# Every layer in two halves of its tokens: attention of the second half beside the first half's projection, the feed-forward by halves

## The reference

```python
x = x + attn_a(layernorm(x))        # causal, 16 heads of 16; x@W1+b1, softmax(mask), @Wp+bp
x = x + ffn(layernorm(x))           # silu(x@wg.T) * (x@wu.T) @ wd.T, hidden 768, int weights / 127
x = x + attn_b(layernorm(x))        # window of 64 keys, 63 given keys ahead of the first token
x = x + ffn(layernorm(x))
# attn_a: w = einsum('bhqd,bhkd->bhqk', q, k) / 4; softmax over the keys up to the query
# attn_b: k_win = k_pad[:, idx] with idx = arange(l)[:, None] + arange(64)[None, :]
```

## Time and profile before

| | us |
|---|---|
| median of 3 runs | 1554.76 (1550.01 to 1557.61) |
| profiled execution, own time | 1558.07 |
| its span in the trace | 1556.3 |
| PE busy / DVE / ACT / POOL | 1312.2 / 965.1 / 756.2 / 390.9 |
| mean granted clock of TensorE | 0.932 of full speed |

### The profile page before, as it was taken

How to read it: one execution, slowest core, us unless ns; L and a number is a source line. 1 busy time by engine, 2 the same in 40 slices (tenths; PEclk the granted TensorE clock), 3 DMA queues, 4 the chain that set the end, 5 groups by cost and what they waited for, 6 DMA issues and landing times.

```text
span 1556.3 us, 23982 instructions
## 1 busy us (share of the span) xinstructions
PE 1312.2 (84%) x9473; PEld 813.8 (52%) x9473; DVE 965.1 (62%) x1564; ACT 756.2 (49%) x1133; POOL 390.9 (25%) x387
## 2 busy tenths in 40 slices
PE   2799879796998987989699997898788988798968
PEld 2533338654763325855584332784477333386547
DVE  5487655556567746555658773665556876555563
ACT  2426654344434675536342667453544266544534
POOL 1302223201330223311242123330134022232013
PEclk9979999998988999999796999999999699999979
DMA  7620120714170021152325011142235201207120
GB/s 290 203 66 16 60 78 30 188 37 139 49 191 2 23 97 62 52 138 73 136 61 145 9 60 62 54 129 63 91 116 138 68 16 57 74 38 186 57 85 28
DMA packets 86335, 134.86 MB, mean 87 GB/s; under 512 B 24176, under 2 KB 59312, under 8 KB 82992
## 3 DMA queue, kind: packets, MB, share of 16 engines
q1 hardware_dynamic: 86208, 133.09, 28.7%
HBM read 51.45 MB, written 11.61 MB: 41 GB/s over the span
## 4 chain that ended last, share of the span: by engine, by line
PE 56%; DVE 20%; ACT 8%; DMA 6%; issue 4%; POOL 4%; SPq 1%; POOLq 0%; ACTq 0%; DVEq 0%
DVE peak L594 13%; PE opsum L1072 11%; PE ring L1045 8%; PE ring L1022 6%; PE ring L1106 6%; PE ring L1107 6%; PE ring L990 5%; ACT probs L835 4%; PE opsum L1120 2%; PE opsum L1123 2%; DMA q_st<-peak_b 2%; PE ring L924 2%; PE ring L925 2%; PE ring L926 2%; PE ring L910 2%
## 5 line engine op out<-in xcount | busy, mean ns | idle before, releaser
L835 ACT ACTIVATE probs<-ring 128x768 f32<-128x768 f32 (+5 forms) x496 | 400.5, 836 | 403.6 <-PE ring L1045 252.2
L594 DVE TENSOR_REDUCE peak<-ring 128x4 f32<-128x768 f32 (+7 forms) x480 | 462.2, 1004 | 166.7 <-PE ring L990 163.5
L1022 PE MATMUL ring<-k_st,q_st 96*128 96x192 bf16 (+4 forms) x1280 | 275.9, 323 | 36.1 <-DVE peak L594 24.4
L1045 PE MATMUL ring<-q_st,k_st 98*128 98x512 bf16 (+5 forms) x1344 | 249.9, 296 | 47.6 <-DMA q_st<-peak_b 24.8
L1072 PE MATMUL opsum<-probs,V 128*32 128x192 f32 (+5 forms) x2816 | 223.6, 411 | 11.1 <-POOL probs L516 9.0
L1045 PEld LDWEIGHTS ring<-q_st,k_st 98*128 98x128 bf16 x1344 | 94.4, 99 | 204.7 <-ACT probs L835 65.9
L1022 PEld LDWEIGHTS ring<-k_st,q_st 96*128 96x128 bf16 x1280 | 99.1, 101 | 159.8 <-DVE peak L594 76.8
L516 POOL TENSOR_SCALAR_AFFINE_SELECT probs<-probs 128x512 f32<-128x512 f32 x128 | 81.2, 634 | 391.1 <-ACT probs L835 391.1
L528 POOL TENSOR_TENSOR h_lo<-hid,h_hi 128x512 fp32r<-128x512 f32 x96 | 123.4, 1289 | 205.1 <-ACT h_hi L869 205.1
L1106 PE MATMUL ring<-xt_hi,w_gu_sb 128*128 128x512 f32 x384 | 154.9, 403 | 21.7 <-issue 18.9
L990 PE MATMUL ring<-mask_a,ident_b 128*128 128x128 bf16 (+2 forms) x704 | 159.9, 280 | 0.0
(11 more groups left out here) (123 smaller groups left out, 1914.7 us busy)
## 6 DMA issues: line engine op xcount, KB each, us to landing
w_gu_sb<-img_gu SPq DMA_DIRECT2D x16, 1536.0 KB, 6.7
w_qkv<-img_qkv SPq DMA_DIRECT2D x8, 1536.0 KB, 7.5
q_st<-q_part SPq DMA_DIRECT2D x96, 128.0 KB, 2.5
q_st<-q_part SPq DMA_DIRECT2D x48, 256.0 KB, 4.6
on_hi<-o_hi SPq DMA_DIRECT2D x64, 128.0 KB, 2.7
k_st<-k_part SPq DMA_DIRECT2D x48, 144.0 KB, 2.5
k_st<-k_part SPq DMA_DIRECT2D x24, 288.0 KB, 7.3
k_st<-k_part SPq DMA_DIRECT2D x48, 128.0 KB, 2.5
```

Of the source, the lines that this page charges most:

```text
L594: dve.tensor_reduce(peak[:, g % 2, :].rearrange("p (h i) -> p h i", i=NT)[:, h:h + heads, i], heads_of(plan.slot[e], unit, plan.a_width(i) ...
L835: act.activation(probs[:, j % 2, h:h + heads, 0:w], heads_of(plan.slot[e], unit, w), ACT.Exp).then_inc(exp_done, 1)
L1022: pe.matmul(flat(plan.slot[e])[:, per * n + c:per * n + c + d], q, k_st[0:SP_ROWS, HG * g + h0 + n, first_key + c:first_key + c + d], star ...
L1045: last = pe.matmul(flat(plan.slot[e])[:, per * n + c:per * n + c + d], kk, q_st[:, HG * g + h0 + n, q0 + c:q0 + c + d], start=(per * n % 5 ...
```

## The change

The unit of attention is now a supergroup (`sg`, 0 to 7): 4 heads and half of the tokens as queries. Groups of the first half come first. In the causal layer the first half sees key tiles 0 to 3, the second all eight; in the sliding layer 0 to 4 (64 rows of tile 4) and 4 to 8.

- `opsum` has one bank per supergroup, by turns. The direct normalisation D is gone: every supergroup goes C, R, M, H, K. `probs` tiles are half as wide.
- N cuts the peaks into a bfloat16 part and a rest before the transpose, so T needs one DVE instruction and one DMA instead of two of each. The values V of four tiles, the projection of four tiles and the residual of two tiles are one unit each, in slots of the ring.
- O of the first half (`O0`) stands inside the attention of the second half. After attention come L2 (transposes for the first half's LayerNorm), gate and up of the first half (G0 to G5), `O1`, down of the first half (W), L3, gate and up of the second half (G6 to G11). Down of the second half is moved into the next layer as `w`, behind its first two Q.
- The order is made by a new `Plan.order`, a list scheduler with a table of durations (`steps`) and one of preferences (`LIKES`), one program for each engine apart. It also fixes which banks of the ring an event gets. PE waits for the earlier holders of exactly these banks.
- ACT's table loads are placed where the next operation of another table follows.

PE at the end of the first sliding layer, before: the last second-pass unit of group 3 (score matmul L1045, mask L990), the weighting by V (L1072), and the first projection tile (L957 to L959).

The diff, cut to its core:

```diff
 RING = 3
-V_FIRST = 4
+SUPERS = 2 * GROUPS
+USES_RING = "QPATBOLG"
+LIKES = (
+    dict(T=1.0, N=1.0, V=0.53, O=0.11, L=0.02, w=2.0, W=0.3, Z=0.15, H=0.26, M=0.77, J=0.05, I=0.2,
...
-        _, self.events = min((self.order(lead) for lead in ahead), key=lambda x: x[0])
+        self.us, self.program, self.banks = self.order(LIKES[0 if self.causal else 1])
...
+    def steps(self, e):
...
+            return [("PE", 0.03 + mask * heads + 0.00043 * w, 0.1), ("DVE", 0.09 + 0.00104 * w, 0.1)]
...
+        if kind == "V":
+            return [("PE", 0.1 + 0.00105 * self.b_width(e[1] // 4, e[2]), 0.15)]
+        if kind in "wW":
+            return [("PE", 4.4, 0.1), ("DVE", 2.1 if self.causal == (kind == "W") else 0.7, 0.1)]
...
+        if kind == "G":
+            k = e[1]
+            gate = [(("I", k - 2), 0)] if k >= 2 else [(("V", 7, self.keys[1][-2]), 0)]
+            return [[(("L", 2 + k // 6), 2), (last_b, 0), (("F", "gu", 1), 0)], gate][step]
...
+                    elif kind == "N":
...
+                        dve.tensor_copy(peak_h[:], peak[:, sg % 2, 0, :]).then_inc(peak_cut, 1)
+                        dve.wait_ge(peak_cut, n + 1)
+                        dve.tensor_tensor(peak[:, sg % 2, 1, :], peak[:, sg % 2, 0, :], peak_h[:],
+                                          ALU.subtract).then_inc(peak_lo, 1)
...
-                    elif kind == "D":
...
-                        dve.reciprocal(osb[:, k, :], osb[:, k, :]).then_inc(direct, 1)
...
+            def slot_free(a, e):
+                for b, (kind, *n) in BEFORE[a, e]:
...
+                    elif kind == "A":
+                        pe.wait_ge(a_max, A_BASE[b] + plan.a_base[n[0]] + n[1] + 1)
...
-                for t in range(4, NT):
-                    project(a, t)
-                    if t == 5:
-                        turn(0, 2 * a + 1)
...
-                pe.wait_ge(gu_in, 32 * (a + 1))
-                for k in range(12):
-                    gate_up(k)
...
-                    if k >= 9:
-                        down(k - 9)
...
+            work = [(a, e) for a in range(LAYERS) for e, step in PLANS[a].program["PE"]]
+            first = [work.index((a, ("G", 0))) for a in range(LAYERS)]
+            last = [work.index((a + 1, ("w", 1, 1))) + 1 for a in range(LAYERS - 1)] + [len(work)]
+            done = 0
+            for n0, n1 in zip(first, last):
+                run(work[done:n0])
                 with pe.If(has_second > 0):
+                    run(work[n0:n1], True)
                 with pe.Else():
+                    run(work[n0:n1], False)
+                done = n1
```

More of the change, by code:

```diff
@@ L695, in _ @@
+            dve.wait_ge(x_in, 16)
+            for m in range(2):
+                for p in range(2):
+                    stats_of(m, p, x_next)
             for n, (_, _, ints) in enumerate(weights):
@@ L761, in _ @@
             for a in range(LAYERS):
-                attention(a)
-                ffn(a)
+                layer(a)
         @block.scalar
@@ L1143, in _ @@
             pe.wait_ge(s_pool, 3)
-            for h in range(2):
-                turn(h, 0)
+            for m in range(2):
+                turn(m, m)
             pe.wait_ge(s_split, 2)
```

1548 lines of the change are left out of this document (849 added, 699 removed), and 5 rows, old and new, of the table w.

## The result

| | before | changed kernel |
|---|---|---|
| median of the runs, us | 1554.82 (1550.01 to 1557.61, 4 runs) | 1571.36 (1568.18 to 1573.12, 4 runs) |
| ratio, 95% interval | | 1.0105 [1.0087, 1.0124] |
| profiled execution, its span | 1558.07, 1556.3 | 1573.12, 1571.4 |
| mean granted clock | 0.932 | 0.949 |
| PE idle (span less busy) | 244.1 | 259.8 |

What follows compares the result with a forecast made beforehand. PE was taken to bound about 1312 us, the rest serial hand-overs at layer seams. Gains of 14 us a sliding and 9 a causal layer, 4 x 23 = 92, took the 1556.3 us span to 1464, put down as 1460, range 1430 to 1490.

Steps and rivals of the forecast that it cites:

- the seam's timetable behind G0: Sliding seam: G0 5.2 us after last V, six G units (9.9 us) cover normalisation, then O1 and W; 9.2 us gained.
- the sliding layers' first scores: Sliding start: two moved down tiles cover the split-and-stack chain, ready about 12.1 us after first Q; PE idle 0.8 us.
- Sliding middle: Saturated stage of sliding attention: pays for 4 extra B units and 4 extra V tiles, 2 us lost.
- they only move: Sliding start: two deferred down-projections, 6.0 us, only move from one layer's end to the next layer's start.
- Causal tail: Causal layer after the last reduction: 20 us of ACT with O0 beside it, 21 us instead of 33.
- The causal middle: Causal attention between start and last reduction: between 106 and 128 us from PE's and DVE's work, taken as 115.
- rival A: Only the seams gain: DVE bounds the causal middle at 128 us instead of 115; 1512 us, chance 0.22 with E.
- Rival D: PE at 1.2 GHz through first halves, +17 us a causal layer; 1528 us, chance 0.05.
- C: Slower: PE waits for slots fixed by a table of assumed durations, 0.54 us a stop; 1590 us, chance 0.08.
- E: Halves do not overlap, O0 and its LayerNorm come late: seam gains about half, 1500 us; chance 0.22 with A.
- The sign set for a wrong forecast: Seam after attention: forecast is wrong if first-half work is spread so that G0 waits over 8 us after last V.
- The clock: Sliding seam stages, granted 0.79 and 0.80 of full speed: less idle there gains some 1.4 us a layer.

Runs made afterwards that it cites:

- h2: Changed kernel with Sqrt table loaded by the root, causal slots renamed, second-half LayerNorm scale and L3 sooner (causal), first q parts sooner (sliding): 1518.70 us, ratio 0.9754.
- f7: Changed kernel with the LayerNorm root's Sqrt table loaded by the root itself, not ahead: 1548.04 us, ratio 0.9963 to the kernel before.
- g3: Changed kernel with the second half's LayerNorm scale and L3 moved sooner in the causal layers: 1565.19 us, ratio 1.0063 to the kernel before.
- f5: Changed kernel with the LayerNorms' square root replaced by a copy and its table loads dropped (output differs): 1547.94 us, ratio 0.9954 to the kernel before.
- e3: Changed kernel with the first half's projection held until after all attention, order made anew: 1615.58 us, ratio 1.0410 to the kernel before.
- h3: h2 with e3's edit, the first half's projection held until after all attention: 1600.14 us, ratio 1.0283 to the kernel before.
- e2: Changed kernel with two slots of the later causal layers renamed, so the first Q does not take L5's: 1557.52 us, ratio 1.0025 to the kernel before.
- g1: Changed kernel with the L2 transposes moved ahead of the last V tiles in every layer: 1576.51 us, ratio 1.0140 to the kernel before.
- h4: h2 plus g1's move of L2, with another slot for L2 in the causal layers: 1515.32 us, ratio 0.9733 to the kernel before.

## Why the prediction was wrong

It expected to gain 92 us in eight layers, and the kernel lost 15 in its trace. By its own stages, from first Q to first exponential, to last reduction, to last V, to next Q (forecast from its working, then the changed kernel, then the four edits of h2):

| us | forecast | changed | h2 |
|---|---|---|---|
| causal: start | 32.0 | 35.9 | 34.9 |
| causal: middle | 115 | 113.3 | 115.5 |
| causal: tail | 21 | 25.1 | 25.0 |
| causal: seam | 39.7 | 45.1 | 40.9 |
| sliding: start (38.8 + 6.0 - 5.4) | 39.4 | 42.8 | 40.9 |
| sliding: middle, with O0 (55.1 + 2 + 2.9) | 60 | 66.2 | 66.1 |
| sliding: seam (64.8 - 6.0 - 2.9 - 9.2 - 1.4) | 45.3 | 50.9 | 42.0 |
| pair | 352 | 379.3 | 365.3 |

The sliding seam's forecast comes out of a difference of totals; by the prediction's own clock times (G6 at 27.4, six units, two transposes) it would be about 39. The layers of h2 (columns as in the earlier trace rows):

```profile
776.10:992.40 216.30, 189.01 (x1252) 101.48 (x1251) 139.18 (x216) 118.01 (x155) 60.36 (x63) 0.96 0.23 70
992.40:1141.40 149.00, 131.89 (x1142) 98.35 (x1141) 85.95 (x184) 76.87 (x122) 35.69 (x30) 0.95 0.34 103
```

**The step that failed: the seam's timetable behind G0** ("Six G units (9.9 us, to 15.1) then cover"). In us after the end of the last V tile, over all eight layers:

| | forecast | changed | h2 |
|---|---|---|---|
| G0 starts | 5.2 | 3.9 to 4.7 | 3.9 to 4.4 |
| six G units last | 9.9 | 12.3 to 13.8 | 12.3 to 13.7 |
| first down starts | 18.0 | 21.9 to 23.6 | 20.4 to 22.1 |
| G6 starts, causal | 27 | 31.7 to 34.4 | 27.2 to 27.6 |
| G6 starts, sliding | 27.4 | 31.3 to 34.7 | 29.9 to 31.7 |

G0 came as forecast. The stop before G6, forecast at 3 and 3.4 us, is 2.5 us in the causal layer and 1.5 in the sliding one. What was put at nothing, or too short, is this:

- The six G units. 9.9 is six times 1.65, the planner's own duration for a unit; at full clock a unit takes 1.82 us in the trace, and behind the stop before G0 the first matmuls run at the lower level of the clock (below).
- The stop before down, 2.4 us, at nothing. 1.5 us of it go when the table load goes from ahead of ACT's copies (f7). The forecast counted the two loads in the causal tail as part of ACT's 20 us, and no other.
- The 4.0 us before the first Q of the later causal layers, at nothing. The forecast spoke of table-given slots for the scores, and here it is the first Q.
- The 4.4 us before the sliding layers' first scores, at 0.8. The stack was there 15.9 us after the first Q and not 12.1.

The working followed one chain and let every other queue be free.

The runs show 23 us for where the loads stand, 14 for the slot and 6 for the root's result waiting in DVE's list, 53 together, against the 111 missed. In the traces (1571.4 to 1520.0 us) 35.8 of them are idle time of PE and 15.6 its busy time, so the clock has a share in each of these prices. In h2 the seams are at 40.9 and 42.0, the causal one 1.2 over its forecast and the sliding one 3.3 under. That closeness is in part luck: the stop before G6 that g3 removes was in the forecast, 3 us a causal layer, and it makes up for six G units that still last 2.4 us or more over the forecast. What was right in the mechanism is that the overlap removes the wait for the projection and that G0 follows the last V tile closely.

**Sliding middle**, 6 us a layer. The forecast charged 2 us for added units. One part is first-pass units that moved. The reductions of the sliding layer by stage, of the kernel before (start, rest) and of the changed one:

```profile
1023.70:1062.50 38.80, 13.21 (x15) 0.97 0.75 189
1062.50:1117.60 55.10, 16.28 (x17) 0.96 0.16 52
```
```profile
1024.50:1067.30 42.80, 7.48 (x8) 0.88 0.41 114
1067.30:1133.50 66.20, 22.78 (x24) 1.00 0.35 106
```

Before, 15 of 32 first-pass units ran in the start, where PE had time; now 8 do, since two supergroups are two half groups. Seven more stand in the middle, at about 0.66 us of PE each (four scores and a mask; an estimate from their distance in the trace), 4.6 us. The step "they only move" was applied to down and not asked of the first pass. But PE's busy time there is 60.31 us, hardly more than the 59.5 that the forecast's 60 contains (its idle time of 0.55 taken off); the stage is granted 1.00 for 0.96 before, which gives some of it back. What the stage has more than forecast is idle time, 5.9 us for 0.55 before: it is not saturated any more. 5.8 of them PE waits before V tiles for exponentials, 15 times, and 2.0 at once behind the two table loads, which f5 takes away.

**Causal tail**, 4 us. Ahead of it ACT is done with supergroup 6, and the last group's first exponential needs transposed peaks, their cut, one DMA and the scores:

```profile
953.03 1.23 DVE L760 TENSOR_REDUCE peak<-ring 128x1 f32<-128x1024 f32 x1 [0.64 <-PE ring L1126]
```
```profile
957.68 0.62 ACT L1017 ACTIVATE o_hi<-onf 128x512 fp32r<-128x512 f32 x1
961.43 2.85 ACT L998 ACTIVATE probs<-ring 128x1024 f32<-128x1024 f32 x3 [3.13 <-PE ring L1170]
```

7.2 us lie between the last reduction and that exponential, and ACT stands for 3.13 of them. The forecast counted ACT's work alone, and ACT's work is as forecast: 19.91 busy us for 20. So the 4 us are ACT's idle time, most of it this hop, and no run took it away. The two table loads among the 20 are worth 2.5 us or so: without them, in f5, the tail is 22.4 us. h2 leaves them where they are, and its tail is 25.0.

**What held.** Waits before the projection vanished, for both halves. The causal middle, the term with the widest bounds, came out at 113.3 for 115: rival A (128, DVE-bound) is refuted, with DVE at 89.75 of 113.30, 0.79. (A's 128 rests on DVE's work of about 110 us; the terms listed for it add up to 106. The three attention stages measured 113.) Rival D too: the four causal starts are granted 0.90 to 0.95 and the middle read here 1.00 (the first 38 us of one other middle 0.88). Nor did C's stops come: PE's own waits of the first-pass scores on "probs" and "peak" are 22.3 and 15.4 us, for 7.5 and 24.4 before, 6 us more in all. (The 76.8 of the earlier trace rows that C priced a stop by is the weight load's wait, PEld; PE's own was 24.4, 60 times.) But C had named the right object, slots given by a table, at the wrong instruction, and the result lies in C's direction. E did not happen, and e3 shows roughly what it would have cost. The sign set for a wrong forecast, G0 over 8 us after the last V tile, did not show although the forecast was wrong; the sliding layer at 159.9 for 145 and the idle time at 259.8 for 150 did.

**The clock**, priced at 1.4 us a sliding layer and at nothing in the causal one, is worth more than that. Behind the 2.46 us stop before G0 shown above, the matmuls of gate and up first follow each other at 0.43 us and then at 0.23:

```profile
985.20 0.63 PE L1237 MATMUL ring<-xt_lo,w_gu_sb 128*128 128x512 f32 x1
985.62 0.63 PE L1236 MATMUL ring<-xt_hi,w_gu_sb 128*128 128x512 f32 x1
...
988.09 0.40 PE L1236 MATMUL ring<-xt_hi,w_gu_sb 128*128 128x512 f32 x1
988.33 0.39 PE L1237 MATMUL ring<-xt_lo,w_gu_sb 128*128 128x512 f32 x1
```

The granted clock is 0.53 from 983.78 to 987.20 and 1.00 from there to 996.20; at the sliding seam it is 0.50 for 6.1 us. At its two levels, the mean granted clock says how long the slow one ran: 2 x (1 - 0.949) x 1571 = 160 us in the changed kernel, 116 in h2 (0.962), 221 in h3 (0.931). From h2 to h3 the slow time grows by 105 us, PE's busy time by 31.4 and its idle time by 47. So an idle microsecond of these seams goes with about 1.7 us of time; from the changed kernel to e2, f7 and h2 it is 1.4 to 1.65, an estimate from one trace each. "TensorE: Matmul & The Clock Gate" of the Trainium skill, section "Part 1: The HAM clock gate", has idle stretches throttle the array; rows agree in that the stages with the stops have 0.87 and 0.88, and the sliding middle, with stops of 0.24 us until its tail, 1.00. The 0.66 of the causal start before is a row on which they do not: PE was busy for 26.88 of 29.40 us there.

What stays open: 53 of the 111 us came back in h2, but a part of them, the stop before G6, was a loss that the forecast had counted. Some 24 (four sliding middles) and 16 (four causal tails) rest on the rows above, and only the part of the table loads in them is touched by a run, f5. The rest is spread over the starts and the longer G units. The stop before G0, 2.5 us a seam, was not removed by any edit, and a move of L2 (g1) only put another stop in its place.

## What to carry to other kernels

Before pricing an overlap, write down for each engine at the seam everything that its queue holds between the two events, table loads and slots included: an item there counts less by its own length than by what stands behind it. In this kernel a table load belongs directly at its user, where the engine waits anyway, and not at the first moment at which it is legal. And an order that was chosen together with wrong durations was not mended by correcting two of them alone (+29 us). The time of the kernel depends on the order by more than the change was worth, so a forecast for a new order needs a timetable of every engine, not of one chain.

## What the runs showed that was not expected

- The number of table loads (1.283 us each) decided nothing, where they stand 23 us: f7 with 52 is as fast as f5 with 16. In the rows shown no more than 0.02 us lie between the last ACTIVATE and a load, or between a load and the next ACTIVATE.
- Renaming two PSUM slots, no instruction or order changed, gave 14 us of 1571.
- The best median, h4 at 1515.32 us (ratio 0.9733 [0.9713, 0.9753]), is 2.7% under the kernel before, with no arithmetic changed; h2, without the move of L2 and its slot, cannot be told from it.
